# A causal convolution on TensorE, from fp32 matmuls to three fp32r passes over split operands

## What is computed

```python
Bq, Hq, Lq = u.shape
mask = (jnp.arange(Lq) < length[:, None]).astype(u.dtype)
u_m = u * mask[:, None, :]
kernel = _get_kernel(log_dt, C, log_A_real, A_imag, Lq)
n = 2 * Lq
k_f = jnp.fft.rfft(kernel, n=n)
u_f = jnp.fft.rfft(u_m, n=n)
y = jnp.fft.irfft(u_f * k_f, n=n)[..., :Lq]
y = y + u_m * D[:, None]
return y * mask[:, None, :]
...
w = _dequantize(qweight, weight_scale, weight_zero_point)
return jnp.einsum('bsk,nk->bsn', x, w) + bias
...
x = x + _L0_ffn_ref(_L0_cond2_ref(x, ...), ...)
```

## Time and profile before

| | |
|---|---|
| median of 3 runs | 882.75 us (879.04 to 883.1) |
| profiled execution | 879.7 us, span 877.9 us |
| PE busy | 820.7 us, 93% of the span |
| DVE busy | 635.5 us, 72% |
| ACT busy | 430.2 us, 49% |
| POOL busy | 287.4 us, 33% |
| chain that ended last | PE 60%, DVE 28%, ACT 8% |
| mean granted clock of TensorE | 0.986 of 2.4 GHz |

### The profile page before, as it was taken

How to read it: one execution, slowest core, us unless ns; L and a number is a source line. 1 busy time by engine, 2 the same in 40 slices (tenths; PEclk the granted TensorE clock), 3 DMA queues, 4 the chain that set the end, 5 groups by cost and what they waited for, 6 DMA issues and landing times.

```text
span 877.9 us, 14236 instructions
## 1 busy us (share of the span) xinstructions
PE 820.7 (93%) x5593; PEld 664.1 (76%) x5593; DVE 635.5 (72%) x1078; ACT 430.2 (49%) x753; POOL 287.4 (33%) x255
## 2 busy tenths in 40 slices
PE   6898999999999998999999999999997699999997
PEld 5776687778778776877787788778675478887886
DVE  3648859977996583558475565946977569999996
ACT  2565647555573766374555736555564322222221
POOL 4001222121122217221212222020110378888883
PEclk9999999999999999999999999999998899999999
DMA  9801010000101010101001010102123025555431
GB/s 240 193 1 25 1 52 4 22 28 26 25 1 52 1 25 1 52 7 23 25 27 26 0 52 1 25 18 59 29 69 120 3 81 146 157 151 153 152 97 73
DMA packets 49570, 49.20 MB, mean 56 GB/s; under 512 B 22192, under 2 KB 32224, under 8 KB 49504
## 3 DMA queue, kind: packets, MB, share of 16 engines
q1 hardware_dynamic: 47232, 47.61, 19.7%
q0 software_dynamic: 1056, 0.49, 0.3%
q10 hardware_dynamic: 1216, 0.19, 0.1%
HBM read 35.61 MB, written 8.47 MB: 50 GB/s over the span
## 4 chain that ended last, share of the span: by engine, by line
PE 60%; DVE 28%; ACT 8%; issue 2%; POOL 1%; DMA 0%; POOLq 0%; ACTq 0%; DVEq 0%
DVE z_low L1249 9%; PE ps L919 8%; PE ps L693 5%; PE ps L573 4%; PE ps L574 4%; PE ps L575 4%; PE ps L694 4%; PE ps L695 4%; PE ps L700 4%; PE ps L699 4%; DVE sc L1225 4%; PE ps L938 3%; PE ps L937 3%; PE ps L592 3%; ACT qt L1020 3%
## 5 line engine op out<-in xcount | busy, mean ns | idle before, releaser
L1020 ACT ACTIVATE qt<-ps,m_bias 128x512 f32<-128x512 f32 x256 | 174.3, 689 | 94.8 <-PE ps L700 93.9
L511 POOL TENSOR_TENSOR pT_low<-pT,pT_high 128x512 fp32r<-128x512 f32 x60 | 80.8, 1347 | 376.1 <-ACT pT_high L1029 376.1
L1249 DVE TENSOR_TENSOR z_low<-ps,z_high 128x512 fp32r<-128x512 f32 x128 | 78.0, 684 | 86.0 <-ACT z_high L1038 85.4
L693 PE MATMUL ps<-q_high,m_high 128*128 128x512 f32 x256 | 105.6, 413 | 12.3 <-ACT qt L1020 9.0
L694 PE MATMUL ps<-q_high,m_low 128*128 128x512 f32 x256 | 100.9, 394 | 0.0
L700 PE MATMUL ps<-q_low,m 128*128 128x512 f32 x256 | 100.9, 394 | 0.0
L695 PE MATMUL ps<-q_high,m 128*128 128x512 f32 x256 | 100.7, 393 | 0.0
L699 PE MATMUL ps<-q_low,m_high 128*128 128x512 f32 x256 | 100.2, 392 | 0.0
L1025 ACT ACTIVATE sc<-sc 128x512 f32<-128x512 f32 x60 | 38.1, 635 | 89.7 <-DVE sc L1231 89.7
L693 PEld LDWEIGHTS ps<-q_high,m_high 128*128 128x128 f32 x256 | 47.9, 187 | 37.4 <-ACT qt L1020 23.7
L919 PE MATMUL ps<-x1T,toep 128*128 128x512 f32 (+3 forms) x256 | 74.3, 433 | 0.0
(11 more groups left out here) (258 smaller groups left out, 1991.3 us busy)
## 6 DMA issues: line engine op xcount, KB each, us to landing
x_in<-in_x SPq DMA_DIRECT2D x16, 512.0 KB, 10.7
x_s<-in_x SPq DMA_DIRECT2D x32, 256.0 KB, 4.3
toep<-taps_scratch SPq DMA_DIRECT2D x32, 256.0 KB, 4.1
out<-res SPq DMA_DIRECT2D x32, 256.0 KB, 2.2
c_tok<-ctok SPq DMA_DIRECT2D x64, 64.0 KB, 2.1
wq_nope<-in_L_attn_Wq_up SPq DMA_DIRECT2D x2, 1536.0 KB, 14.4
wq_rope<-in_L_attn_Wq_up SPq DMA_DIRECT2D x4, 384.0 KB, 14.1
qw<-in_L_ffn_qweight SPq DMA_DIRECT2D x1, 768.0 KB, 4.6
```

Of the source, the lines that this page charges most:

```text
L511: pool.tensor_tensor(flat(pT_low_of(u)[:, n]), flat(pT_of(u)[:, n]), f(flat(pT_high[:, n])), ALU.subtract).then_inc(s["pl_done"], 1)
L693: pe.matmul(out_, m0_high[:, q, cols], q0_high[:], start=True, stop=False)
L1020: act.activation(qt[:, j, :], ps[:, BT + j % 2, :], ACT.Identity, bias=m_bias[:, h:h + 1]).then_inc(s["qt_done"], 1)
L1249: dve.tensor_tensor(part(z_low), ps[:, ZBANK[n][e], :].rearrange("p (b a c) -> p b a c", b=2, a=GP), f(part(z_high)), ALU.subtract).then_i ...
```

## The change

The taps are split into `taps_high` (rounded to fp32r) and `taps_low` (the rest) by two more ops of DVE in unit 8, and stored in two DRAM tensors, each behind its own zeros. Each channel loads two Toeplitz tiles in place of one. The turned input is evicted by ACT as `x1T_high`, in fp32r, and DVE subtracts it from PSUM into `x1T_low`. The convolution runs through `three`, so as 12 fp32r matmuls. The two tiles have one more block of 128 columns ahead, which POOL fills with zeros once; the last of the four steps takes that block too, and so writes 256 columns in place of 128. Tiles move to make room, with no more of them in a ring than before; x_s of channel 4 is loaded after the attention's end in place of before it.

```diff
@@ sync
-            sp.dma_start(scratch_taps[:, 0:KPAD], zero[:]).then_inc(s["taps_stored"], 16)
+            for n in range(2):
+                sp.dma_start(scratch_taps[n][:, 0:KPAD], zero[:]).then_inc(s["taps_stored"], 16)
...
-                    sp.wait_ge(s["taps_done"], 3)
-                    sp.dma_start(scratch_taps[:, KPAD:KPAD + T].rearrange("h (a c) -> a h c", a=LA),
-                                 taps).then_inc(s["taps_stored"], 16)
+                    sp.wait_ge(s["taps_done"], 5)
+                    for n, part in enumerate((taps_high, taps_low)):
+                        sp.dma_start(scratch_taps[n][:, KPAD:KPAD + T].rearrange("h (a c) -> a h c", a=LA),
+                                     f(part)).then_inc(s["taps_stored"], 16)
...
             def load_toep(c):
-                src = bass.AP(scratch_taps.tensor, c * KROW, [[1, P], [1, T]])
-                sp.dma_start(toep[c % R][:], src).then_inc(ring_toep[c % R], 16)
+                for part, tile in ((0, toep_high[c % R]), (1, toep_low[c % R])):
+                    src = bass.AP(scratch_taps[part].tensor, c * KROW, [[1, P], [1, T]])
+                    sp.dma_start(f(tile[:]), src).then_inc(ring_toep[c % R], 16)
@@ gpsimd
+            for tile in x1T_high + x1T_low:
+                pool.memset(f(tile[:, 0, :]), 0.0).then_inc(s["x1T_zero"], 1)
             pool.wait_ge(s["bias2_in"], 32)
@@ tensor
             def convolved(c):
...
                 for e in range(TT):
-                    mm = pe.matmul(ps[:, 4 + q, e * P:T], toep[c % R][:, e * P:(e + 1) * P],
-                                   x1T[q][:, 0:TT - e, :].rearrange("p t b -> p (t b)"), start=(e == 0),
-                                   stop=(e == TT - 1))
+                    first, last = (1, TT + 1 - e) if e < TT - 1 else (0, 2)
+                    out_ = ps[:, 4 + q, (TT - last + first) * P:T]
+                    rows = slice(e * P, (e + 1) * P)
+                    high, low = (tile[q][:, first:last, :].rearrange("p t b -> p (t b)") for tile in (x1T_high, x1T_low))
+                    mm = three(out_, toep_high[c % R][:, rows], toep_low[c % R][:, rows], high, low, e == 0, e == TT - 1)
@@ scalar
-                    act.wait_ge(s["taps_stored"], 16)
+                    act.wait_ge(s["taps_stored"], 32)
...
-                    act.copy(x1T[q][:].rearrange("p t b -> p (t b)"), ps[:, 2 + q, :]).then_inc(s["x1T_done"], 1)
+                    act.copy(x1T_high[q][:, 1:, :].rearrange("p t b -> p (t b)"),
+                             ps[:, 2 + q, :]).then_inc(s["x1T_high_done"], 1)
@@ vector
+                    dve.wait_ge(s["taps_done"], 3)
+                    dve.tensor_copy(taps_high, taps).then_inc(s["taps_done"], 1)
+                    dve.wait_ge(s["taps_done"], 4)
+                    dve.tensor_tensor(taps_low, taps, f(taps_high), ALU.subtract).then_inc(s["taps_done"], 1)
...
                 if c % 4 == 1 and c // 4 + 1 < C // 4:
                     split(c // 4 + 1)
+                if 0 <= c - 1 < C:
+                    q = (c - 1) % 2
+                    dve.wait_ge(s["x1T_high_done"], c)
+                    if c - 1 >= 2:
+                        dve.wait_ge(s["conv_ready"], c - 2)
+                    dve.tensor_tensor(x1T_low[q][:, 1:, :].rearrange("p t b -> p (t b)"), ps[:, 2 + q, :],
+                                      f(x1T_high[q][:, 1:, :]).rearrange("p t b -> p (t b)"),
+                                      ALU.subtract).then_inc(s["x1T_done"], 1)
```

More of the change, by code:

```diff
@@ L128, in build @@
     mem = Memory(nc)
-    scratch_taps = nc.dram_tensor("taps_scratch", (C, KROW), F32, kind="Internal").ap()
+    scratch_taps = [nc.dram_tensor(f"taps_scratch{n}", (C, KROW), F32, kind="Internal").ap() for n in range(2)]
     ps = mem.ctx.enter_context(nc.psum_tensor("ps", [P, 8, 512], F32))
@@ L149, in build @@
     ctok = t("ctok", [P, 2, 4, KVL], F32R)
[L150 to L153, removed]
     KB = 1024
+    q_at = m.room(8 * KB)
+    q0_high = t("q0_high", [P, ST], F32R, at=q_at)
+    q0_low = t("q0_low", [P, ST], F32R, at=q_at + 2 * KB)
+    q1_high = t("q1_high", [P, ST], F32R, at=q_at + 4 * KB)
+    q1_low = t("q1_low", [P, ST], F32R, at=q_at + 6 * KB)
     mix_at = m.room(1 * KB)
@@ L234, in build @@
     taps = theta[0:LA, :, 0:LC]
+    taps_high = theta[0:LA, :, LC:2 * LC].bitcast(F32R)
+    taps_low = taps.bitcast(F32R)
     turns = o_sum[:, :, 48:64].rearrange("p (h x) c -> p h x c", x=4)
@@ L256, in build @@
     z_row = t("z_row", [P, T], at=m0l_at + 5 * KB)
[L257 to L260, removed]
+    x_s = [t(f"x_s{n}", [B, T], at=(m1_at + n * 2 * KB if n < 4 else zh_at + 8 * KB if n == 4 else
+                                    m0l_at + 14 * KB if n == 5 else zh_at + (2 * n - 12) * KB)) for n in range(RX)]
+    toep_high = [t(f"toep_high{n}", [P, T], F32R,
+                   at=(m0h_at + (8 + 2 * n) * KB if n < 4 else m0l_at + (8 + 2 * n - 8) * KB)) for n in range(R)]
+    toep_low = [t(f"toep_low{n}", [P, T], F32R,
+                  at=(q_at + 2 * n * KB if n < 4 else (m1_at + 14 * KB, m0l_at + 12 * KB)[n - 4])) for n in range(R)]
     bo = t("bo", [P, T], at=m1_at + 8 * KB)
@@ L266, in build @@
     o_low = [t(f"o_low{n}", [VH, 4, B], F32R, at=qt_at + (8 + 2 * n) * KB) for n in range(2)]
-    x1T = [t(f"x1T{n}", [P, TT, B], at=qt_at + (12 + 2 * n) * KB) for n in range(2)]
-    y = [t(f"y{n}", [P, TT, B], at=qt_at + (16 + 2 * n) * KB) for n in range(2)]
-    y_high = [t(f"y_high{n}", [P, TT, B], F32R, at=qt_at + (20 + 2 * n) * KB) for n in range(2)]
+    x1T_high = [t(f"x1T_high{n}", [P, TT + 1, B], F32R, at=qt_at + 12 * KB + 2560 * n) for n in range(2)]
+    x1T_low = [t(f"x1T_low{n}", [P, TT + 1, B], F32R, at=qt_at + 17 * KB + 2560 * n) for n in range(2)]
+    y = [t(f"y{n}", [P, TT, B], at=zl_at + 2 * n * KB) for n in range(2)]
+    y_high = [t(f"y_high{n}", [P, TT, B], F32R, at=zl_at + (4 + 2 * n) * KB) for n in range(2)]
     y_low = [t(f"y_low{n}", [P, TT, B], F32R, at=qt_at + (24 + 2 * n) * KB) for n in range(2)]
@@ L284, in build @@
     ffn_names = "ffn_in wo_in len_in one_ready row_in wf_ready wfT_ready wfT_done c_done woT_ready woT_high_done woT_done".split()
-    channel_names = ("bias2_in xb_done oh_done ol_done a_ready x1_done x1b_done b_ready x1T_done conv_ready y_done "
+    channel_names = ("bias2_in xb_done oh_done ol_done a_ready x1_done x1b_done b_ready x1T_zero x1T_high_done x1T_done conv_ready y_done "
                      "yh_done yl_done f_ready f_taken sum_taken x1s_done res_done").split()
@@ L392, in _ @@
             sp.wait_ge(s["t_ready"], GH * NU)
-            sp.wait_ge(s["taps_stored"], 32)
+            sp.wait_ge(s["taps_stored"], 64)
             sp.dma_start(bo[:], d["L0_attn_bo"].partition_broadcast(P)).then_inc(s["bias2_in"], 16)
@@ L415, in _ @@
                 load_toep(c)
-                if c >= 4:
+                if c == 5:
                     load_x1(c)
             sp.wait_ge(s["out_done"], NU)
-            for c in range(R, RX):
+            for c in (4,) + tuple(range(R, RX)):
                 load_x1(c)
@@ L914, in convolved @@
                 pe.wait_ge(s["x1T_done"], c + 1)
-                pe.wait_ge(ring_toep[c % R], 16 * (c // R + 1))
+                if c == 0:
+                    pe.wait_ge(s["x1T_zero"], 4)
+                pe.wait_ge(ring_toep[c % R], 32 * (c // R + 1))
                 if c >= 2:
@@ L1047, in output @@
                     act.wait_ge(s["taps_ready"], 2)
-                    act.wait_ge(s["taps_stored"], 32)
+                    act.wait_ge(s["taps_stored"], 64)
                 first = 16 * k + 8 * n
```

## The result

The changed kernel takes **887.1 us** (median of 7 runs, 885.46 to 888.6), the kernel before in the same session 882.64 us (7 runs, 879.04 to 884.21). The ratio is 1.006 with an interval of 1.0041 to 1.0079: slower, clear of the noise but by little, just at the prediction's own mark of 0.5% (887.2). The forecast was no change at 881 us. 887.1 lies inside the stated range of 876 to 890. The slip, the rival with a chance of 0.25, had 887.

A forecast was written before the change was run, and what follows sets the result against it. The prediction took PE to bound the channel loop at 5.20 us a channel, with DVE 8% behind. Cycle and end gains together of 2.1 us, off the 882.75 us median, gave 880.6, say 881 us; range 876 to 890.

The forecast's parts named there:

- The slip: Channel loop rival: y_low beats DVE's scale-and-add in step three, which takes 6.02 us; 887 us, chance 0.25 whole or in part.
- Point 1: Convolution on PE: 12 one-pass matmuls take 1.94 us instead of 2.16, so PE's channel falls by 0.22 to 4.98.
- Point 2: DVE in each channel: the added subtraction takes 0.60 us of start spacing, making the normal step 4.80 us.
- Point 3: Every fourth channel, with o_low: DVE's o_low waits for POOL's x_s + bo, so the step takes 5.87 us.
- Point 4: Four-channel cycle: 5.87 + 4.80 + 4.98 + 4.98 = 20.63 us against 20.80, L1518 taken to win; with the end, 2.1 us gained.
- The third step: Third channel of the cycle: L1518 and y_low nearly tie; with L1518 winning it takes PE's 4.98 us.
- Points 5 to 8: First channels, taps' split, start's second zeros store, doubled Toeplitz loads: each counted as nothing, the store between nothing and 1 us.
- DVE as a plain bound: Channel loop rival: DVE's 4.80 busy plus 0.60 gives 5.40 us a channel; 889 us, chance 0.1 shared with late loads.
- PE's gain in full: Channel loop rival: no o_low delay or slip, each channel 4.98 us, 7 us less; 876 us, chance 0.15, in full or nearly.

The follow-up runs named there:

- e8_order: Changed kernel with o_low moved behind x1T_low and two POOL operations (y_low, x1 + fb) held by semaphore waits; 878.94 us, ratio 0.9974.
- e9_psum: Changed kernel with the product of projection and s_row written to PSUM, where the last addition reads it; 877.85 us, ratio 0.9963.
- e2_olow: Changed kernel with DVE's o_low moved behind x1T_low in every fourth channel; 884.63 us, ratio 1.0042.
- e1_tie: Changed kernel with one wait replaced, so POOL's y_low starts only after DVE has scaled the preceding channel's FFN result; 882.53 us, ratio 1.0019.
- e6_one_load: Changed kernel loading one Toeplitz tile a channel, the high one serving as the low one too; 887.9 us, ratio 1.0061.
- e4_pe_alone: Changed kernel without DVE's subtraction, ACT writing the rounded turned input into both tiles; 881.2 us, ratio 1.0002.
- e5_sub_alone: Kernel before with only DVE's subtraction added, into a spare tile that the convolution waits for; 886.86 us, ratio 1.0053.
- e10_psum_before: Kernel before with the product of projection and s_row written to PSUM, where the last addition reads it; 881.96 us, ratio 1.0012.
- e7_no_bo: Changed kernel without POOL's addition of the output bias; 878.04 us, ratio 0.9952.

## Why the prediction was wrong, point by point

- **Point 1, PE's convolution at 1.94**: right (1.94 in the chain). PE's channel of 4.98 is shown by e8_order's steps 3 and 4 (4.98); over whole cycles of e9_psum it is 5.01.
- **Point 2, the subtraction and the normal step of 4.80**: right (0.68 recorded, 0.60 apart; steps of 4.82 and 4.84).
- **Point 3, the o_low step of 5.87**: right (5.90; o_low 1.18, expected about 1.15), and e2_olow shows that the wait for POOL is its cause.
- **Point 4, the cycle**: this is the step that failed, and in one sentence: "I therefore take L1518 to win." The third step was to take 4.98 us and took 6.06. The gap was computed as 0.03 in favour of y_low, and the traces show 0.00 to 0.03. What I held against it, that POOL takes the port about 0.1 after its recorded start, does not hold for these two: y_low won at each of those gaps. e1_tie shows that the rest of the working was sound: with the order turned round the cycle is 20.72 us, where the prediction had 20.63. And the answer stood in the trace of the kernel before, in an early cycle that I had not looked at; timelines of DVE and POOL there:

```profile
732.28 1.79 DVE L1518 SCALAR_TENSOR_TENSOR x_s<-c_row,y_sum,x_s 128x512 f32<-128x512 f32 x1
```

```profile
732.25 1.27 POOL L566 TENSOR_TENSOR y_low<-y,y_high 128x512 fp32r<-128x512 f32 x1
```

The very gap of 0.03, and y_low first. From two rows I had bounded the switching point between L1518 0.06 ahead (it won) and 0.16 behind (it lost) and argued inside it; this row stands just at the computed gap. With y_low first the prediction's own rival gives 5.87 + 4.80 + 6.02 + 4.80 and 887 us, and the chip gave 5.90 + 4.84 + 6.06 + 4.82 and 887.1. That the rival's time comes out to 0.1 us is luck: it had a cycle 0.69 us longer seven times, 4.8 us, where it was 0.84 us (20.78 to 21.62) six times, 5.1; it took 0.5 off for the end, which cost 0.65; it had no term for the 0.6 us around the span; and the part ahead of the loop scatters by more than any of these. The Trainium skill's SBUF — State Buffer, in its section on the two separate sides, has the pair locked by whichever starts first for the whole instruction; taken to the letter it gave that number. The trace agrees with the lock (1.84 us for 0.74), but not on who started first at this precision: in two of the six cycles DVE's operation is recorded in the same hundredth of a us or just ahead, and y_low still wins. I had the rule and weighed an inference from two recorded durations above it.
- **Points 5 to 8** (first channels, the taps' split, zeros, loads): nothing, as predicted. After the taps' two operations (0.68 and 1.22) DVE still waits 9.33 us, had 11.36; e6_one_load puts the second load at 0.07 us of the loop, though a load of the low part lands in 5.4 us instead of 4.1. The DMA engines' share is 0.84, not the 0.72 that I had computed from the number of transfers; nothing waited for it. The zeros were not separated from the scatter of the start.
- **The rivals.** The slip came true. "DVE as a plain bound" (889) fell: DVE's waiting is not a constant per channel, and e8_order takes 1.4 us out of each cycle without taking out any work. "PE's gain in full" (876) is nearly where e9_psum ends, 877.85, though against its own kernel before that is 2.9 us less and 4.8 in the loop, not 7. The o_low step does find POOL's port free there (0.68), but the last addition had to leave the port first.
- **What was missing among the arguments**: e4_pe_alone. I held that slips in the kernel before cost nothing, "since PE needs 5.20 anyway". True, but it does not follow that a shorter PE channel is worth anything: slips and the waits around them held the cycle at the same 20.8 us. Even had the subtraction been free, the change would have brought next to nothing and not 7 us.

The sum of the loop, by steps: 24 steps (six cycles) take 129.72 us instead of 124.66, +5.06. The first five steps and the lead-in give 0.46 back, the last two steps and what follows the last x1 cost 0.65. Together +5.25. The last part is where a term of mine was wrong too: I expected the last channels to gain 0.22 each and the last convolution 0.2, and they lost. In the trace the scale-and-add meets y_low twice there (1.38 and 1.41 us, where it took 0.74 in the kernel before); whether that is all of it was not tried. The prediction also counted seven cycles, and only six repeat.

## What to carry to other kernels

Where two engines share a port, read for each operation not only how long it is but which other one it meets, and compute the gap between the two starts; a sum of busy times said 92% here and hid slips of 1.1 us, which cost nothing until one more operation of 0.6 us left no time to make up for them. If the gap comes out below 0.1 us, look through the whole trace for the same two at the same gap; without one, give both outcomes like chances, or better, fix the order with a semaphore or take one of the two off the port (an input in PSUM), which brought 8.6 and 10 us of loop here. And before counting a gain on the bounding engine, ask what cycle the others would have if it were faster.

## What the runs showed of the hardware

- **Where a close race for the shared pair turns.** For the scale-and-add against y_low, over all traces: DVE's operation won whenever it was recorded 0.04 us or more ahead; y_low won all 35 meetings in which DVE's was recorded from 0.01 ahead to 0.04 behind, and those where it came later still. No meeting fell between. It is no rule for every two operations: o_low, recorded 0.00 to 0.02 behind POOL's x1 + fb, won nine times and lost three. So a recorded order of starts within 0.02 us does not tell who wins. The loser pays 1.1 us on DVE (1.84 for 0.74) and 0.5 us on POOL (1.82 for 1.29).
- **DVE's operations on PSUM and one SBUF tile were not held up by POOL.** y = convolution times mask starts within 0.04 us of POOL's x1 + fb 122 times over all traces, and always takes 0.67 to 0.68 us, POOL's 1.27 to 1.30. Writing the product to PSUM instead of SBUF costs 11 ns (689 against 678).
- **Three fp32r matmuls against one in fp32**: 12 matmuls, 3 x 1408 columns with the widened tile, take 1.94 us where the 1280 columns in fp32 took 2.16. The convolution gains 10%, PE's channel 4%, and it costs an operation on another engine.
- **Left open**: what lies around the span is 1.8 us in the kernel before, e5_sub_alone and e10_psum_before, and 2.3 to 2.5 in most kernels with the three passes, e6_one_load among them (2.1 in e4_pe_alone, 1.9 in e7_no_bo). It is 0.6 us of the change's cost, and its cause stays open.
